# First layer by tokens: x stationary and base moving, weight reads put ahead, two corrected blocks

## What is computed

```
layer one:  ae = layernorm(cond) * g + b          # 8 x 512
            h  = gelu(ae @ w1 + b1)               # 8 x 512
            xw = h @ w2 + b2                      # w2: 512 x 8192, 16 MB
            x_a, x_b = halves of xw, each 512 x 8 for every block
            layer[b] = base + x_a[b] @ x_b[b].T   # 512 x 512, a rank 8 term for each block
            x1 = x + (x + x @ layer[b])           # = x @ (2 I + base + x_a x_b^T)
layer two:  shared = (silu(x1 @ W1) * (x1 @ W3)) @ W2          # 512 -> 1024 -> 512
            s = sigmoid([x1, cond] @ router_W); top 2 of 8 experts by s + bias, gates normed
            routed = sum over the 2 experts of gate * gelu(x1 @ W1e) @ W2e
            out = x1 + (shared + routed) / 3
```

## Time and profile before

| what | us |
|---|---|
| median of three runs | 1096.06 |
| the profiled execution, by its own time | 1096.63 |
| its span in the trace | 1094.4 |
| TensorE busy, all of the span | 1067.4 |
| DVE / ACT / POOL busy | 484.3 / 399.5 / 153.5 |

### The profile page before, as it was taken

The page is one execution under the profiler, slowest core; times in us unless marked ns, Lnnn a source line. Parts: engine busy times, 40 slices in busy tenths (PEclk is TensorE's granted clock), DMA queues, the critical chain, the costliest instruction groups (busy, mean ns, idle before and its releaser), DMA issues.

```text
span 1094.4 us, 15374 instructions
## 1 busy us (share of the span) xinstructions
PE 1067.4 (98%) x5226; PEld 871.9 (80%) x5226; DVE 484.3 (44%) x1026; ACT 399.5 (37%) x687; POOL 153.5 (14%) x193
## 2 busy tenths in 40 slices
PE   7998899979999999999999999999999999999998
PEld 6666687868888888888888888888888888888887
DVE  3104654633523665566556645335413333242435
ACT  3212344542123665666566656312112121111211
POOL 2002176650000000000000000142020202002020
PEclk9999999989999999999999999999999999999999
DMA  8862589771792677887676565554232313123131
GB/s 300 306 245 92 181 324 346 266 272 58 209 253 61 202 238 216 250 267 217 189 219 211 155 187 194 184 164 155 90 103 77 115 36 120 36 77 115 38 115 38
DMA packets 134490, 189.36 MB, mean 173 GB/s; under 512 B 9503, under 2 KB 77087, under 8 KB 132919
## 3 DMA queue, kind: packets, MB, share of 16 engines
q1 hardware_dynamic: 122902, 154.28, 44.3%
q0 software_dynamic: 11552, 34.61, 9.5%
HBM read 115.99 MB, written 72.88 MB: 173 GB/s over the span
## 4 chain that ended last, share of the span: by engine, by line
PE 79%; issue 1%; ACT 0%; DVE 0%; ACTq 0%
PE K L1541 10%; PE K L1542 10%; PE K L1543 10%; PE M L1541 5%; PE M L1542 5%; PE M L1543 5%; PE Rb L1541 5%; PE L L1541 5%; PE Rb L1542 5%; PE L L1542 5%; PE Rb L1543 5%; PE L L1543 5%; ACT x1tok L877 0%; ACT L484 0%; DVE gTl L503 0%
## 5 line engine op out<-in xcount | busy, mean ns | idle before, releaser
L484 ACT ACTIVATE slf<-K 128x512 f32<-128x512 f32 x64 | 38.2, 598 | 204.5 <-PE K L1543 203.6
L1541 PE MATMUL M<-w2h,gTh 128*128 128x512 f32 x256 | 100.5, 392 | 6.0 <-DVE gTl L503 6.0
L489 ACT CAST gTh<-slf 128x512 fp32r<-128x512 f32 x64 | 39.8, 621 | 179.3 <-DVE slf L499 177.7
L1542 PE MATMUL M<-w2l,gTh 128*128 128x512 f32 x256 | 100.3, 392 | 0.0
L1543 PE MATMUL M<-w2h,gTl 128*128 128x512 f32 x256 | 100.1, 391 | 0.0
L826 POOL DMA_INDIRECT yb<-ys_d,pos_fix x64 | 61.6, 962 | 274.4 <-DVE total L1469 203.0
L499 DVE TENSOR_TENSOR slf<-L,slf 128x512 f32<-128x512 f32 x32 | 22.1, 690 | 147.4 <-PE L L1543 130.3
L1541 PE MATMUL K<-x1h,w13h 128*128 128x512 f32 x224 | 87.1, 389 | 0.0
L1542 PE MATMUL K<-x1l,w13h 128*128 128x512 f32 x224 | 87.1, 389 | 0.0
L1543 PE MATMUL K<-x1h,w13l 128*128 128x512 f32 x224 | 87.1, 389 | 0.0
L1401 DVE TENSOR_TENSOR e2l<-e2raw,e2h 128x512 fp32r<-128x512 f32 x64 | 41.3, 686 | 81.4 <-ACT e2h L980 81.4
(11 more groups left out here) (275 smaller groups left out, 2502.5 us busy)
## 6 DMA issues: line engine op xcount, KB each, us to landing
w2c<-in_L_cond_w_dram SPq DMA_DIRECT2D x8, 2048.0 KB, 8.7
e1raw<-in_L_cond_W1e_dram SPq DMA_DIRECT2D x16, 1024.0 KB, 7.3
e2raw<-in_L_cond_W2e_dram SPq DMA_DIRECT2D x16, 1024.0 KB, 5.4
xr<-xs_d SPq DMA_DIRECT2D x64, 256.0 KB, 4.5
ys_d<-yo SPq DMA_DIRECT2D x32, 512.0 KB, 7.3
xtok<-in_x_dram SPq DMA_DIRECT2D x32, 256.0 KB, 5.3
x_d<-x1tok SPq DMA_DIRECT2D x8, 1024.0 KB, 9.2
xs_d<-zeros SPq DMA_DIRECT2D x8, 1024.0 KB, 8.4
```

Source lines behind the costliest of these rows:

```text
L484: nc.scalar.activation(slf[:, h % 2], U[h % 2][:], ACT.Silu).then_inc(ffn.silu, 1)
L489: nc.scalar.copy(gTh[:, h % 2], slf[:, h % 2]).then_inc(ffn.g_hi, 1)
L1541: mm(o, ah, bh_, start=start, stop=False)
L1542: mm(o, ah, bl_, start=False, stop=False)
```

## The change

- **Operands.** In the first layer x becomes the stationary operand and base the moving one, so a result stands by tokens, in a bank per tile t. `base_bank`, `base_half`, `base_rows`, `low` and `corr` change their operands. base and the rank 8 factors are stored with their columns in another order (`(c j f)` to `(j c f)`), the order in which x1tok is kept.
- **Removed.** `tok` (128 transposes on the TensorE), xp, the stores to and reads from x1T_d, and the casts of blocks 6 and 7 from xp.
- **In their place.** The block that the shared network takes first (6) is transposed once more (`turn_held`, 16 transposes, with a second copy by ACT, heldtok). Block 7 is stored, read back in quarters (keptq) and turned by DVE (`turn_kept`), then cut behind part 6 of `ffn(S, 0)`. Blocks 0 to 5 are read in quarters from x1_d (`load_quarters`, four transfers for one) and turned by DVE (`turn_block`) inside the block before.
- **Order of the first layer.** `EARLY` = 2: only blocks 0 and 1 are corrected afterwards. On the TensorE the `cond_net` 2 to 5 follow one another with little between them, and the base products of block 2 go behind the scores and between the corrections. On SP `load_net(5)` goes ahead of the reads of x for block 2. `load_factors` for blocks 5, 6 and 7 stands between the scatters of POOL.
- **Buffers.** Every block has an x1tok of its own. Before the first silu ACT now waits only `tok_left(act, 2)`.
- **DVE in `ffn(S, 0)`.** `turn_kept` stands behind part 5, the cut of block 7 behind part 6, and `tables` behind part 7.
- **The last `rank`** moves into the first up part of `ffn(S, 0)`.

The core of the diff:

```diff
-    EARLY = 3
+    EARLY = 2
-            return M[o] if b == 0 else M[(b * KC + o) % 2]
+            n = b * TT + t
+            return M[n % 2] if b == 1 else M[n % 4]
@@ base_half
-                    mm(bank[:], bh[:, c, cols], xh[:, c], start=(c == 0), stop=False)
-                    mm(bank[:], bh[:, c, cols], xl[:, c], start=False, stop=False)
-                    last_mm = mm(bank[:], bl[:, c, cols], xh[:, c], start=False, stop=(c == KC - 1 and b < EARLY))
+                    mm(bank[:], xh[:, c, rows], bh[:, c], start=(c == 0), stop=False)
+                    mm(bank[:], xl[:, c, rows], bh[:, c], start=False, stop=False)
+                    last_mm = mm(bank[:], xh[:, c, rows], bl[:, c], start=False, stop=(c == KC - 1 and b < EARLY))
@@ TensorE, new
+            def turn_held(t):
+                pe.wait_ge(held_f, t + 1)
+                k_free(pe, "held", HELD, t)
+                bank = k_bank("held", HELD, t)
+                for c in range(KC):
+                    last_mm = nc.tensor.transpose(bank[:, c * P:(c + 1) * P], heldtok[:, t, c * P:(c + 1) * P], ident[:])
+                last_mm.then_inc(held_ps, 1)
@@ TensorE, corrections
             scores(0)
-            xtr(3, 0)
-            xtr(3, 1)
+            scores(1)
             corr(0, 0)
             corr(0, 1)
-            scores(1)
+            base_half(2, 0, 0)
             corr(0, 2)
             corr(0, 3)
+            base_half(2, 0, 1)
             corr(1, 0)
             corr(1, 1)
-            tok(0, 0)
-            tok(0, 1)
-            scores(2)
+            base_half(2, 1, 0)
             corr(1, 2)
             corr(1, 3)
+            base_half(2, 1, 1)
@@ ACT, ahead of ffn(S, 0)
             cut_piece(2)
-            for t in range(TT):
-                keep_tok(NB - 1, t)
-            tok_left(act, 4)
-            tok_left(act, 5)
+            tok_left(act, 2)
@@ DVE, behind parts of ffn(S, 0)
-            after[6] = lambda: tables(dve)
-            after[7] = lambda: (rows_in_ys(dve), gate_weights(dve))
+            between = {5: turn_kept, 6: cut_kept}
+            for h in between:
+                after[h] = lambda h=h, was=after.get(h, lambda: None): (was(), between[h]())
+            after[7] = lambda: (tables(dve), rows_in_ys(dve), gate_weights(dve))
@@ SP, weights and x
-            for n in range(2, 5):
+            for n in range(2, 6):
                 load_net(n)
             for t in range(TT):
                 load_x(2, t)
-            for n in range(5, LOADS):
+            for n in range(6, LOADS):
                 load_net(n)
@@ SP, behind the last group
-            sp.dma_start(x1raw[:], x1T_d[:, 0:1, :].rearrange("p b n -> p (b n)")).then_inc(x1raw_in, 16)
+            def load_quarters(b):
+                alone(sp)
+                rows = quarters(b)
+                for j in range(4):
+                    sp.dma_start(xq[32 * j:32 * j + 32].rearrange("p t i f -> p (t i) f"), rows[j]).then_inc(xq_in, 16)
+            load_quarters(0)
@@ DVE, layer two
+            def turn_block(b):
+                dve.wait_ge(xq_in, b * 64 + 64)
+                if not first(b):
+                    dve.wait_ge(xf_hi, b * KC)
+                for t in range(TT):
+                    nc.vector.transpose(x1raw[:, :, t].rearrange("p c (i n) -> p i c n", i=4),
+                                        xq[:, t].rearrange("p i (c f) -> p i c f", c=KC)).then_inc(xq_turned, 1)
+            turn_block(0)
             cut_block(0)
             start_sum(KEPT, 0)
-            ffn_dve(dve, F, 0, {2: lambda: end_sum(0), 5: lambda: whole_sum(HELD, 1, comb)})
+            ffn_dve(dve, F, 0, {2: lambda: end_sum(0), 3: lambda: turn_block(1), 5: lambda: whole_sum(HELD, 1, comb)})
             with dve.Fori(1, NF - 1) as b:
-                ffn_dve(dve, F, b, {2: lambda: end_sum(b + 1)})
+                ffn_dve(dve, F, b, {2: lambda: end_sum(b + 1), 4: lambda: turn_block(b + 1)})
```

More of the change, by code:

```diff
@@ L1012, in _ @@
             act.sem_inc(y_sb, Y_FREE)
-            act.wait_ge(x1_out[TOK_BUFFER[HELD]], 16)
+            act.wait_ge(x1_out[HELD], 16)
             cut_x(0, 2)
@@ L1236, in _ @@
             xt_lo_(1, 3)
-            for t in range(TT):
-                xt_lo_(2, t)
             dve.wait_ge(cond_ps, LOADS)
@@ L1331, in _ @@
             st_lo(1)
-            turn(1)
             add_low(1, 0)
             add_low(1, 1)
+            turn(1)
             add_low(1, 2)
@@ L1337, in _ @@
             add_condition(0)
-            st_lo(2)
-            turn(2)
-            xt_lo_(3, 2)
-            xt_lo_(3, 3)
-            for o in range(KC):
-                add_low(2, o)
             for b in range(EARLY, NB):
@@ L1378, in _, with turn_kept, cut_kept @@
             cut_piece(2)
+            def turn_kept():
+                dve.wait_ge(kept_in, 64)
+                for t in range(TT):
+                    nc.vector.transpose(keptT[:, :, t].rearrange("p c (i n) -> p i c n", i=4),
+                                        keptq[:, t].rearrange("p i (c f) -> p i c f", c=KC)).then_inc(kept_turned, 1)
+            def cut_kept():
+                for c in range(KC):
+                    dve.wait_ge(x1_hi, c + 1)
+                    tt(x1l[:, c], keptT[:, c].rearrange("p t n -> p (t n)"), x1h[:, c].bitcast(F32),
+                       ALU.subtract).then_inc(x1_lo, 1)
             def turn_rows(g, t):
@@ L1592, in low @@
-            def low(b, o, bank, start):
+                if c > 0:
+                    pe.wait_ge(base_lo, c + 1)
+                    for t in range(TT):
+                        rows = slice(t * P, (t + 1) * P)
+                        mm(M[t][:], xh[:, c, rows], bh[:, c], start=False, stop=False)
+                        between(t, 0)
+                        mm(M[t][:], xl[:, c, rows], bh[:, c], start=False, stop=False)
+                        between(t, 1)
+                        last_mm = mm(M[t][:], xh[:, c, rows], bl[:, c], start=False, stop=(c == KC - 1))
+                        if c == KC - 1:
+                            last_mm.then_inc(main_ps, 1)
+                        between(t, 2)
+                    return
@@ L1594, in low @@
+                pe.wait_ge(base_hi, 1)
+                for a, w, ready in ((xh, bh, lambda t: pe.wait_ge(xt_hi, t + 1)), (xl, bh, lambda t: pe.wait_ge(xt_lo, t + 1)),
+                                    (xh, bl, lambda t: pe.wait_ge(base_lo, 1))):
+                    for t in range(TT):
+                        ready(t)
+                        mm(M[t][:], a[:, c, t * P:(t + 1) * P], w[:, c], start=(a is xh and w is bh), stop=False)
+            def low(b, t, bank, start):
                 pe.wait_ge(s_lo, b + 1)
```

538 lines of the change are left out of this document (230 added, 308 removed).

## The result

The changed kernel takes 1083.1 us in the median of four runs (1079.66 to 1083.53), the kernel before 1096.11 (1092.36 to 1100.91, four runs). The ratio of the runs is 0.9872, 95% interval 0.9828 to 0.9916: faster by 1.3%. The forecast was 1074, between 1064 and 1081. The sign was right, the gain too large by 9.1 us.

What follows compares the result with a forecast made beforehand. The TensorE was taken to bound the kernel. First layer -25.0, shared blocks +1.9 and hand-over +1.1 sum to -22.0 us: from 1096.63, by the median, 1074 us. Its own range was 1070 to 1078, the 8-in-10 range 1064 to 1081.

Steps and rivals of the forecast that it cites:

- First layer up to block 3: Start to first scores 83.5 us instead of 98.09, then corrections to block 3's scores 24.4 instead of 18.57.
- Blocks 3 to 7: Block 3's scores to the first shared matmul: five blocks without `tok` take 79.6 us instead of 95.80.
- The 8.1 us of the first silu: Shared blocks: 5.99 us idle and 2.1 of low clock vanish, as ACT waits for block 2's scatters, not block 5's.
- The table: Second shared block, sums of part 3: table made behind part 7 comes late, 7.1 us wait plus 2.1 of clock.
- Rival A: Shared blocks: the table is in time and nothing replaces the 8.1 us saved; -31.2 us, 1065 us; chance 0.15.
- Weight pieces: Shared blocks: piece 5 waits for block 7's store and read-back, yet is cut before it is needed; 0, up to 3 us.
- Hand-over: Start of the last six blocks: quarters, DVE turns and ACT casts delay the first matmul by 1.1 us, bounds 0 to 6.9.
- Transposes: First layer, TensorE: a group of four costs its spacing, 0.43 us, so the 112 that go net are worth 12.0 us.
- Rival D: First layer: transposes are worth their mean duration, 30.6 us in place of 12.0, giving 1055 us; chance 0.02.
- Rival B: First layer: late weights or quarters, or low clock in the corrections, take back 4 to 8 us; 1078 to 1082; chance 0.18.
- Rivals C and E: First: turning x bounds the last blocks, slower than before, chance 0.03. Second: new order fails, no change, chance 0.02.

Runs made afterwards that it cites:

- e1: Changed kernel with the SB factors of blocks 5, 6 and 7 loaded one block of scatters earlier: 1077.65 us, 3.6 less than the changed kernel run again.
- e6: The kernel before, nothing altered, for a second profile: 1092.14 us in ten runs, where 14 other runs of it in that set have 1097.36.
- e5: Changed kernel with ACT waiting for block 5's scatters and store before the first silu, not block 2's: 1081.55 us, against 1081.3 for the changed kernel.
- e2: Changed kernel with the group table made behind part 6 of the first shared block, not part 7: 1073.83 us, 7.5 less than the changed kernel again.
- e0: The changed kernel again, no edit: 1081.29 us (1080.7 to 1082.42).
- e3: Changed kernel with block 7's tokens read back behind weight piece 8 instead of ahead of piece 5: 1080.8 us (1077.68 to 1081.78).
- e7: e4 with each of the 28 groups of transposes of x of blocks 1 to 7 made twice: 1076.66 us, 11.1 over e4.
- e10: e4 with the table behind part 4 and transposes of the identity at the start: 1082.09 us, beside 1082.52 for e4 in that set.
- e4: Changed kernel with the edits of e1, e2 and e3, and ACT freeing its first bank before casting x: 1065.55 us; 1082.52 on another chip.
- e9: e4 with 38 transposes of the identity on the TensorE at the start: 1083.22 us, beside 1082.52 for e4 in that set.

## Why the prediction was right and wrong

**First layer up to block 3: right.** 83.5 and 24.4 us were forecast, 82.00 and 24.02 measured, 1.9 better; the two waits of the corrections came at the places named and within 0.15 us. The weights were in time, but by luck. I worked out 5 us of slack from a median landing of 8.7 us, and in the changed kernel the median is 12.1. The last two eighths were issued at 46.6 and 51.5, landed 13.6 and 13.8 us later, and were used at 60.48 and 65.90: 0.3 and 0.6 us of slack. Why they landed later than before is not shown.

**Blocks 3 to 7: the step that failed.** I priced the TensorE's program (15.7 us a block, 16.06 with a `rank`; 15.59 and 16.02 came) and asked of each other engine only whether it is busy. The queue of GpSimd I did not list, though the section on the change says that factor loads stand between its scatters; their landing stands in the sum as nothing, without a reason. Before, its program loads the factors of six blocks ahead of the first scatter (`range(EARLY + 3)`), in the changed kernel of five, and block 5's load falls behind 16 scatters, which start when the first ranks are there (120.67) and take 1.27 us each. Before, it went out at 138.35, ahead of all scatters, and was needed 5.1 us behind 158.30, at 163.44. Now it goes out at 140.79 and is needed 5.0 us behind the scores of 138.07; the TensorE got on at 146.73. The old issue, in the trace of before:

```profile
138.35 1.03 POOL L782 DMA_DIRECT2D SB<-xwh_d  x2 [13.49 <-PE M L1596]
```

The load even waits for nothing when its turn comes. Price 3.47 us idle and 1.78 at low speed, shown by e1: 5.27.

**The 8.1 us of the first silu: a term of one profile, taken for one of the kernel.** "So 8.1 goes" stands in the sum as if each run of before had it. e6 shows a run in which the idle time is 0.5, and 17 of 39 runs have times like its own. Nor is it shown that it went by waiting for block 2 in place of block 5, as I wrote: e5 waits for block 5 and loses nothing. It does not show the opposite either. The scatters do not run ahead in it, as the second theory of e5 has it, but their completion was quick, 5.3 us as in the quick run of before (5.0), and with 9.8 us the first sums would have waited some 4 us, an estimate from these rows. All five runs of e5 lie within 0.6 us, so none of them shows that case, and what the new wait is worth then stays open. Against the faster runs of before, the change makes the shared blocks 10.5 us longer (131.47 to 142.00), and its whole gain is some 10 us (the lower group of before in the first set, 1091.1 to 1092.3, against 1081.29).

**The table: right.** 7.1 us idle and 2.1 of clock were forecast, 5.30 and 1.9 came, at the place named, and e2 took them away again for 7.5. The 5.30 are less than 7.1 because the TensorE came to these sums 104.7 us behind T and not 100.7, and ACT had e1raw at 106.0 and not 103.9. Rival A is out.

**Weight pieces: mis-sized.** The forecast was "0, with up to 3"; 1.94 us came, and 1.32 in e0. Piece 5 was to be cut 19 us behind T, and came 22.8 behind it (213.30), because the read-back of block 7 stood before it. e3 shows it in the profile.

**Hand-over: right in size, 1.41 against 1.1.** The quarters landed slower than the 4.5 us of xr that I took: DVE started at 677.01, 7.0 us behind the first issue (670.06), where I had 6.0. Since they went out 10.6 us ahead of the last group's end (680.68), this was cheap. That xr has the same form did not make it the same transfer: xq's median is 7.3. The Trainium skill ("DMA: Bandwidth & Descriptors", Bandwidth) wants 1 MiB or more per transfer. My estimate from it was 7.6 us, and the 7.0 lie between that and my 6.0. (It would have put the sum 3.1 us higher by the 4.5 used there, not 2.9.) But these rows do not show that the size did it: x1raw, a block by channels in one transfer of 1 MB, had a median of 7.2 us before (4.7 to 8.1), and xq in quarters has 7.3 (3.4 to 8.8). The 4.8 us that I set against the rule was the landing of one transfer, near the shortest of its kind.

**Transposes: right.** e7 gives 0.44 us for four, where the sum had 0.43. Rival D is out by the time and by this row; the 273 ns are a latency.

**Rival B** came closest: 1078 to 1082 was its range, 1083.1 and 1081.3 were measured. Its mechanism in general, transfers and clock taking back part of the first layer, is what happened, but at none of the places that it names: the weights were in time, the clock was full in the corrections (1.00), and what came late were the factors. I gave it 0.18 and should have given it more, with one look at which transfers stand behind the scatters. Rivals C and E were wrong: the turning of x in the last blocks costs nothing (395.25 against 395.10), and the order does what it says.

## What to carry to other kernels

When the bounding engine gains 20 us, write down for every transfer behind it, on every queue, when it goes out and when it is now needed; a constant that shrinks (here a count of loads ahead of the scatters) moves one as surely as an edit of its line. A single stall of one profile is not a term: profile the kernel before twice, and if its times lie in two groups, find the stall that makes them. A wait and the slow clock behind it are one price where the clock falls (3.47 with 1.78, 5.30 with 1.9; 1.94 cost none), and such losses add up when their causes differ: four small moves gave 15.7 us where 15.7 were worked out, term by term within 1.2. A term that came out right is looked at too: the weights here had 0.3 us left of the 5 forecast.

## What was not expected of the hardware

- The same program took 3% longer in the third set, on another chip, than in the others (before 1128.96 against 1092.3 and 1097.4). In the four profiles of that set TensorE, ACT and DVE stand for up to 17.5 us between 172 and 197 us, while GpSimd issues a scatter every 1.27 us. In three of them ACT stands longest (17.05, 16.38 and 15.67 us), with a releaser that the profile does not place; in e10 DVE stands for 17.53. There is no profile of the kernel before in that set. The Trainium skill ("Runtime: NRT & Kernel Launch", Instruction fetch mechanics) calls instruction fetch mostly hidden but for taken branches. The program has none in this stretch. The instruction queues moved the same bytes in both of e4's profiles (0.34 and 0.11 MB), which does not tell whether fetch was late. The cause stays open.
- In the first microseconds the TensorE can run at half speed while the profile grants it 1.00: in e9, 24 transposes from 1.73 us on took 5.38 us, 0.22 each, where later ones start 0.09 to 0.11 apart.
- Small factor loads behind indirect scatters still landed soon. Block 5's, with scatters ahead of it and behind it, landed in 3.3 to 4.2 us, and the loads of SB as a whole in 1.9 to 4.5; what was late was the issue.
